# Cross attention on one core: weights five turns behind the scores, four pairs of transposed buffers, contexts loaded in six pieces, the query bias loaded as rows

## The reference

```python
q = (pre_q @ Wq + bq).reshape(b, ql, H, D_Q)          # 16 x 100 x 16 x 64
k = (pre_k @ Wk + bk).reshape(b, kl, H, D_Q)          # 16 x 1444 x 16 x 64
v = (pre_k @ Wv + bv).reshape(b, kl, H, D_Q)
scores = jnp.einsum('bqhd,bkhd->bhqk', q, k) / jnp.sqrt(jnp.float32(D_Q))
attn = jax.nn.softmax(scores, axis=-1)
ctx = jnp.einsum('bhqk,bkhd->bqhd', attn, v).reshape(b, ql, H * D_Q)
out = ctx @ Wo + bo
x = pre_q + out                                       # then a layer norm over the 128 columns
return (x - mu) * jax.lax.rsqrt(var + EPS) * gamma + beta
```

## Time and profile before

| | us |
|---|---|
| median of three runs (lowest, highest) | 870.35 (869.59, 874.36) |
| the profiled execution, its own time | 871.59 |
| its span | 869.8 |
| PE busy in the span | 846.3 (97%) |
| DVE busy | 774.7 (89%) |
| ACT busy | 779.6 (90%) |
| POOL busy | 569.1 (65%) |

### The profile page before, as it was taken

One profiled execution on the slowest core, in us unless ns is written; L12 is line 12 of the kernel. 1 busy time (PEld: TensorE's weight loads), 2 busy tenths in 40 slices (PEclk: granted clock), 3 DMA queues, 4 the chain that ended last, 5 costly groups with the idle time before them and its releaser, 6 DMA issues.

```text
span 869.8 us, 19632 instructions
## 1 busy us (share of the span) xinstructions
PE 846.3 (97%) x7306; PEld 605.2 (70%) x7306; DVE 774.7 (89%) x938; ACT 779.6 (90%) x1132; POOL 569.1 (65%) x575
## 2 busy tenths in 40 slices
PE   7999999999999999999999999999999999999996
PEld 6676776767677766777667776776767777677675
DVE  4988888999989989999899998999899999999984
ACT  5899999989999989999989999998989989999983
POOL 2283997949566693867749586694956669397301
PEclk9999999999999999999999999999999999999999
DMA  7899999999999999999999999999999999999985
GB/s 198 186 211 192 195 210 189 216 200 223 215 209 217 217 204 224 209 226 211 205 213 221 216 208 229 198 227 217 213 215 220 205 233 208 222 188 217 209 183 117
DMA packets 683939, 180.80 MB, mean 208 GB/s; under 512 B 654596, under 2 KB 683076, under 8 KB 683844
## 3 DMA queue, kind: packets, MB, share of 16 engines
q1 hardware_dynamic: 682372, 179.01, 105.7%
q10 hardware_dynamic: 1344, 0.53, 0.3%
q0 software_dynamic: 128, 0.01, 0.0%
HBM read 15.35 MB, written 0.82 MB: 19 GB/s over the span
## 4 chain that ended last, share of the span: by engine, by line
PE 52%; ACT 14%; DVE 13%; DMA 8%; issue 7%; SPq 4%; ACTq 0%; POOLq 0%; POOL 0%; DVEq 0%
PE ps L670 25%; PE ps L631 22%; DMA pt_hi<-p_hi 7%; DVE p_lo L932 6%; ACT p L1072 6%; ACT p_hi L1080 5%; DVE nmax L917 4%; SPq L429 2%; PE ps L495 2%; PE ps L488 2%; SPq L420 1%; ACT unused L1023 1%; DMA bq_pairs<-in_L_xattn_bq_dram 1%; DVE rsum L923 1%; ACT o_t L1110 1%
## 5 line engine op out<-in xcount | busy, mean ns | idle before, releaser
L932 DVE SCALAR_TENSOR_TENSOR p_lo<-p,rinv,p_hi 128x1444 f16<-128x1444 f32 x200 | 370.9, 1855 | 7.5 <-ACT p_hi L1080 7.0
L917 DVE TENSOR_REDUCE nmax<-ps 128x1 f32<-128x1446 f32 x200 | 330.0, 1650 | 18.8 <-PE ps L631 18.3
L1080 ACT ACTIVATE p_hi<-p,rinv 128x1444 f16<-128x1444 f32 x200 | 300.0, 1500 | 32.1 <-DVE rinv L925 28.5
L1072 ACT ACTIVATE p<-ps,nmax 128x1446 f32<-128x1446 f32 x200 | 292.2, 1461 | 17.8 <-DVE nmax L917 15.4
L670 PE MATMUL ps<-pt_hi,c_hi 128*128 128x256 f16 (+1 forms) x1232 | 252.9, 261 | 11.4 <-DMA pt_hi<-p_hi 9.0
L670 PE MATMUL ps<-pt_hi,c_lo 128*128 128x256 f16 (+1 forms) x1232 | 253.0, 261 | 0.0
L631 PE MATMUL ps<-ct_hi,g_hi 128*128 128x482 f16 (+3 forms) x624 | 155.5, 367 | 0.8 <-DVE g_lo L892 0.7
L631 PE MATMUL ps<-ct_lo,g_hi 128*128 128x482 f16 (+3 forms) x624 | 154.9, 366 | 0.0
L631 PE MATMUL ps<-ct_hi,g_lo 128*128 128x482 f16 (+3 forms) x624 | 154.9, 366 | 0.0
L670 PEld LDWEIGHTS ps<-pt_hi,c_hi 128*128 128x128 f16 x1232 | 114.1, 98 | 50.4 <-issue 16.8
L1204 POOL TENSOR_TENSOR g_raw<-g_raw,gb_b 128x400 f32<-128x400 f32 x60 | 81.0, 1350 | 96.2 <-ACT g_raw L1096 96.2
(11 more groups left out here) (138 smaller groups left out, 863.0 us busy)
## 6 DMA issues: line engine op xcount, KB each, us to landing
c_raw<-in_ctx_dram SPq DMA_DIRECT2D x32, 256.0 KB, 6.1
pt_hi<-p_hi SPq DMA_TRANSPOSE x200, 3.5
pt_lo<-p_lo SPq DMA_TRANSPOSE x200, 3.7
c_raw<-in_ctx_dram SPq DMA_DIRECT2D x16, 192.0 KB
c_raw<-in_ctx_dram SPq DMA_DIRECT2D x48, 18.0 KB
out_dram<-late_sb SPq DMA_DIRECT2D x16, 50.0 KB
x_sb<-in_x_dram SPq DMA_DIRECT2D x1, 600.0 KB
o_t<-in_L_xattn_Wq_dram SPq DMA_DIRECT2D x2, 256.0 KB, 4.5
```

The costliest lines, as they stand in the source:

```text
L917: dve.tensor_reduce(nmax[:, n % RING:n % RING + 1], ps[:, bank:bank + 3, 0:KEYW], AX.XY, ALU.max, negate=True).then_inc(s_nm, 1)
L932: dve.scalar_tensor_tensor(out=p_lo[:, n % LOS, 0:KL], in0=p32[:, n % P32S, 0:KL], scalar=rinv[:, i:i + 1], in1=p_hi[:, par, 0:KL], op0=AL ...
L1072: act.activation(p32[:, n % P32S, :].rearrange("p (k w) -> p k w", w=KEYW), ps[:, bank:bank + 3, 0:KEYW], ACT.Exp, bias=nmax[:, i:i + 1], ...
L1080: act.activation(p_hi[:, par, 0:KL], p32[:, n % P32S, 0:KL], ACT.Copy, scale=rinv[:, i:i + 1]).then_inc(s_hi, 1)
```

## The change

- `LAG` goes from 4 to 5: PE weighs a unit one turn later, and ACT takes the result one turn later. `PTS` goes from 3 to 4, a fourth pair of transposed buffers. The loop of PE runs on three turns after the last scores instead of two.
- A context is loaded in `NL` = 6 pieces of `TL` = 2 tiles, at r = 0 to 5 (before: three pieces of four tiles at r = 1 to 3); the three tail copies come with the last piece. Each half has its own semaphore, so that a sum waits for its half alone.
- The places in a window move: `CHI_AT` from (4, 6, 7) to (5, 6, 7), `SUM_AT` from (5, 8) to (8, 9), `TOTAL_AT` from 9 to 10, `STORE_AT` from 2 to 10. The sum over x moves from turns (9, 10) to (4, 10).
- Before the loop: the query bias is loaded as 8 rows of 128 (`bq_rows`), the first DMA on ACT's queue, ahead of Wk; PE transposes it ahead of the weights, and DVE copies it into `bq_pairs`. PE makes the second half of the head products ahead of the bias. ACT empties both of its banks (`J_B` was DVE's); DVE takes over the first x (`J_X`) and `gb_sb` from ACT.

```diff
-    LAG = 4
+    LAG = 5
-    PTS = 3
+    PTS = 4
-    LOADS = 6
+    TL = 2
+    NL = KT // TL
-    LOAD_AT = 1
-    STORE_AT = 2
-    CHI_AT = (4, 6, 7)
+    LOAD_AT = 0
+    STORE_AT = 10
+    CHI_AT = (5, 6, 7)
-    SUM_AT = (5, 8)
-    TOTAL_AT = 9
+    SUM_AT = (8, 9)
+    TOTAL_AT = 10
...
+        bq_rows = sb("bq_rows", [PAIRS, P])
-        s_c = [sem(f"context_loaded{i}") for i in range(2)]
+        s_c = [[sem(f"context_loaded{i}_{half}") for half in range(SUMS)] for i in range(2)]
+        s_bqt = sem("bq_turned")
+        s_bqp = sem("bq_pairs_ready")
-        J_A, J_X, J_B = 4, 6, 7
-        J_G = J_B + 2
+        J_A, J_B, J_X = 4, 6, 8
+        J_G = J_X + 1
-        BY_SCALAR = [1, 3, J_A, J_A + 1, J_X, J_B + 1, J_V1, J_M2]
+        BY_SCALAR = [1, 3, J_A, J_A + 1, J_B, J_B + 1, J_V1, J_M2]
-        X_SUM_AT = (9, 10)
+        X_SUM_AT = (4, 10)
...
+            def load_context(b, i):
+                load_tiles(b, TL * i, TL * (i + 1), s_c[b % 2][i * SUMS // NL])
...
-                if LOAD_AT <= r < LOAD_AT + NT and w + 2 < B:
+                if LOAD_AT <= r < LOAD_AT + NL and w + 2 < B:
...
+            pe.wait_ge(s_bq, 16)
+            pe.transpose(ps[:, JOB_BANK, 0:PAIRS], bq_rows[:, :], ident[0:PAIRS, 0:PAIRS]).then_inc(s_bqt, 1)
...
             head_products_by_two(w_t[0], w_t[1], 0, J_A)
+            pe.wait_ge(s_bqp, 2)
+            head_products_by_two(w_t[0], w_t[1], 2, J_B)
             query_bias(take(J_X))
             spread_context_max(job_bank(J_G + 2), 0)
             transpose_x(0, J_X).then_inc(s_fill, 1)
-            head_products_by_two(w_t[0], w_t[1], 2, J_B)
...
-            for n in range(N + 2):
+            for n in range(N + LAG - 2):
...
+            dve.wait_ge(s_bqt, 1)
+            dve.wait_ge(s_bqz, 1)
+            for i in range(2):
+                rows = slice(HEAD_DIM * i, HEAD_DIM * i + HEAD_DIM)
+                dve.tensor_copy(bq_pairs[rows, :, i], ps[rows, JOB_BANK, 0:PAIRS]).then_inc(s_bqp, 1)
...
-            empty(J_B)
+            empty(J_X)
+            dve.tensor_scalar(gb_sb[:, :], job_bank(J_X)[:, XG * QL:XG * QL + H], SCALE, None, ALU.mult).then_inc(s_gb, 1)
...
+            act.dma_start(bq_rows[:, :], bq.rearrange("(c p) -> c p", p=P)).then_inc(s_bq, 16)
...
-            act.wait_ge(s_bqz, 1)
-            for i in range(2):
-                rows = slice(HEAD_DIM * i, HEAD_DIM * i + HEAD_DIM)
-                act.dma_start(bq_pairs[rows, :, i:i + 1], bq.rearrange("(c i p o) -> i p c o", i=2, p=HEAD_DIM, o=1)[i],
-                              allow_slow_non_contiguous=True).then_inc(s_bq, 16)
...
-            for k in (1, 3, J_A, J_A + 1):
+            for k in (1, 3, J_A, J_A + 1, J_B, J_B + 1):
                 empty(k)
             a_sum(0)
-            empty(J_X)
-            act.activation(gb_sb[:, :], job_bank(J_X)[:, XG * QL:XG * QL + H], ACT.Copy, scale=SCALE).then_inc(s_gb, 1)
```

More of the change, by code:

```diff
@@ L353, in every_other, with context_landed @@
             return slice(first, first + 2 * HG - 1, 2)
-        def context_landed(b):
-            return 16 * LOADS * (b // 2 + b % 2)
+        def context_landed(b, half):
+            return 16 * (NL // SUMS + (3 if half == SUMS - 1 else 0)) * (b // 2 + b % 2)
         def emptied(eng, k):
@@ L371, in _, with load_tiles @@
         def _(sp):
[L372 to L377, removed]
+            def load_tiles(b, a, e, landed):
+                par, whole = b % 2, min(e, KT - 1)
+                sp.dma_start(c_raw[:, par, a:whole, :],
+                             ctx_in[b:b + 1, a * P:whole * P, :].rearrange("o (t p) d -> p (o t) d", p=P)).then_inc(landed, 16)
+                if e == KT:
                     tail = ctx_in[b:b + 1, (KT - 1) * P:KL, :].rearrange("o p d -> p o d")
@@ L386, in _ @@
             for g in range(NT):
-                load_context(0, g)
+                load_tiles(0, TG * g, TG * (g + 1), s_cf[g])
             sp.dma_start(x_sb[:, 0:XG, :], x[0:XG, :, :].rearrange("b q d -> q b d")).then_inc(s_x[0], 16)
@@ L391, in _ @@
                 sp.dma_start(w_raw[2][:, cols], Wv[:, cols]).then_inc(s_w[2][half], 16)
-            for g in range(NT):
-                load_context(1, g)
+            for i in range(NL):
+                load_context(1, i)
             def transpose_context_hi(b):
@@ L539, in query_bias @@
             def query_bias(bank):
-                pe.wait_ge(s_bq, 32)
+                pe.wait_ge(s_bqp, 2)
                 for c in range(PAIRS):
@@ L837, in context_max @@
             def context_max(g):
-                dve.wait_ge(s_cf[g], 16 if g < NT - 1 else 16 * (LOADS - NT + 1))
+                dve.wait_ge(s_cf[g], 16 if g < NT - 1 else 16 * 4)
                 dve.tensor_reduce(c_max[:, g:g + 1], c_raw[:, 0, TG * g:TG * g + TG, :].rearrange("p t d -> p (t d)"),
@@ L1025, in context_sum @@
             def context_sum(b, i):
+                act.wait_ge(s_c[b % 2][i], context_landed(b, i))
                 if i == 0:
-                    act.wait_ge(s_c[b % 2], context_landed(b))
                     act.wait_ge(s_cm, b)
@@ L1038, in a_sum @@
                            ax_parts[:, 0, i:i + 1])
-            for k in (1, 3, J_A, J_A + 1):
+            for k in (1, 3, J_A, J_A + 1, J_B, J_B + 1):
                 empty(k)
             a_sum(0)
-            empty(J_X)
-            act.activation(gb_sb[:, :], job_bank(J_X)[:, XG * QL:XG * QL + H], ACT.Copy, scale=SCALE).then_inc(s_gb, 1)
             for g in range(NT):
                 context_hi(0, g)
-            empty(J_B + 1)
             for g in range(NG):
```

## The result

The changed kernel takes **877.1 us** in the median of 16 runs (870.8 to 883.3), the kernel before 871.8 (869.0 to 876.5) beside it: ratio 1.0054, 95% interval 1.0035 to 1.0074. Timed again later in the study it gave 874.0 beside 871.7, ratio 1.0043 (1.0020 to 1.0066). Ratios leave out slow runs, over 1.5% above the fastest of their kernel, which only two kernels further down have. So the change makes the kernel about 4 us slower. The forecast was 863.2, with a range up to 869.5: the sign was wrong and the time lies outside the range.

The account below looks back on a forecast made before the run. PE was taken as the bound, with 10.4 us of pt_hi waits to gain; -10.4 - 0.8 + 3.2 + 0.5 = -7.5 us gave 862.9, taken as 863.2 us, range 859.5 to 869.5.

Parts of the forecast that it names:

- All 12 stalls go: -10.4 us: Middle of the loop: with LAG 5 and four buffers PE no longer waits for pt_hi, saving 10.4 us.
- the sums' +0.5: Sums at r = 8 and 9: ACT falls back 1.0 us, slack shrinks to nearly nothing; +0.5 us, between 0 and 7.
- What is late next?: Middle, once the stalls are gone: no wait from the four buffer pairs; next is the exponentials' slack, usually least 1.1 us.
- So the lateness is SP's backlog after the loads: Middle: pt_hi comes late because SP issues its transposes late behind other DMAs, not for shortage of ACT or DVE.
- the gain is given back: Rival, middle: late transposes hold ACT's p_hi, PE stalls at its scores, 7 us come back: 869 to 870; chance 0.17.
- Before the loop: -0.8: Start: c_hi and g_lo come sooner, so the first scores do too; -0.8 us, between 0 and -2.0.
- the cover: Before the loop: 1.3 us of PE idle time to absorb weights' transposes starting some 1.2 us late if the rows land late.
- Nothing starts sooner: Turn 4: its 18 matmuls go, but the projection still waits for DVE's scale; 1.97 us of weighing move to the end.
- the clock rival: Rival: TensorE's clock falls behind holes at the end and in turn 4, costing 1.7 to 3.3 us: 864.9 to 866.5; chance 0.15.
- The end, +3.2: After turn 199 starts: PE idles 3.1 us for ACT's copy into o_t, the last unit begins later; +3.2 us.
- Pieces, store and sums at nothing and +0.5: Loop: six load pieces and the moved store cost nothing; sums at r = 8 and 9 cost 0.5 us.
- ACT as the bound: Rival: neighbouring sums and columns at r = 9 delay exponentials past slack; at 1.0 us a window, 876; chance 0.07.

Follow-up runs that it names:

- the combination: Changed kernel with the old start, three p_hi buffers, ACT's last but one copy moved earlier, contexts in three spaced pieces from GpSimd's queue: 863.9 us, ratio 0.9918.

## Why the prediction was wrong, point by point

- **"All 12 stalls go: -10.4 us." Half right.** This term is the step that failed: with the sums' +0.5 the middle was to shorten by 9.9 us and did by 2.2, which is 7.7 of the 11.0 us between the forecast sum (-7.5) and that of the stages (+3.5, below). The stalls for `pt_hi` went. The middle gained 5.0 and 4.4 us in the two profiles of the changed kernel against the one of before. Over five profiles of its loop (798.8 to 802.6, mean 800.2) and three of the loop before (799.7 to 803.9, mean 802.4) the gain is 2.2 us. What the stalls cost was itself read from one profile: a second of the loop before has the same (8.2 us in 12 places of the middle), a third, with the rows behind Wk, 4.7 in 10. The mechanism, and about its size, are borne out by the combination: its middle is 10.8 us shorter than in the profile of the kernel before, 9.3 shorter than the mean of the three. What failed is the question that follows, "What is late next?": it looked at the four pairs of transposed buffers and at the exponentials, and left out the two `p_hi` buffers, which were named only as a rival. In their place the runs show ACT waiting 15.0 us for transposes and PE 4.6 us in the middle for ACT's copy behind it; with a third buffer the first is gone, and in the combination taking it away brings 11.0 us of it back.
- **"So the lateness is SP's backlog after the loads." Half right.** With SP relieved and the pieces spaced, the waits stayed at 7.3 us of 9.0. SP's queue is one part, the landing beside the loads' traffic the other. What the fifth turn gives is room for either.
- **The rival "the gain is given back" (0.17)** had the mechanism: late transposes hold ACT by `p_hi`'s two buffers. It put PE's stall at the scores, for the exponentials; it came at the weighing, for `o_t` (4.6 us of the 6.9 lie in the middle), since ACT's copy stands next behind `p_hi` in its order. Its forecast of 869 to 870 lies 1 to 2 us under the first profiled run and 4 to 8 under the medians, as the start and turn 4 were not in it.
- **"Before the loop: -0.8", bounds 0 to -2.0. Wrong in sign**: +2.1 on the mean of nine profiles each. The step that failed is the bound of 0 for the worst case: nothing in the working made a start slower. What came is the slow pace of the head products in six of nine starts. It weighs more where the change put both halves of them ahead of the bias and the spread of the maximum, and so filled the 1.3 us of idle time that was to be the cover. Overlooked too was what the rows push back. It was asked when they land (they were there by 4.3 us and cost nothing), but they are first on ACT's queue: Wk starts at 1.36 us instead of 0.75, and its second half lands at 7.3 to 9.1 instead of 6.0 to 6.3. Whether this brings the slow pace stays open.
- **"Nothing starts sooner" in turn 4: right, but not free.** The projection started at 38.32 as forecast. The hole of 2.8 us cost 0.2 us where the clock stayed up and 1.9 where it fell behind (12.1 against 10.26 us for turns 4 and 5), which it did in seven of the thirteen profiles with five turns. That is the clock rival, priced at 1.7 and given 0.15. The sum itself gave the hole no cost.
- **The end, +3.2: right in kind**, 0.8 too high; +2.4 measured, with the stall at the place named, 2.29 us for 3.1.
- **Pieces, store and sums at nothing and +0.5: borne out** within what can be measured; undoing pieces and store gave 1.0048 and undoing the sums 1.0044, beside 1.0043 and 1.0054.
- **ACT as the bound (0.07): did not come.** The slower side came by the start, the turn-4 hole and the end instead, +2.1, +1.2 (mean of thirteen) and +2.4, which with -2.2 in the middle make +3.5 us. The two ratios give +3.7 and +4.7. The last us is open: the timed runs of the changed kernel spread over 12 us, and only two of them have a profile.

## What to carry to other kernels

Slack between two engines can be no longer than the fewest buffers on the way allow; here it was the two ahead of the DMA. Before a lag is lengthened, list every buffer from the producer on, those ahead of the DMA too, and lengthen them together. Ask of a small load put first in a queue what it pushes back: here 4 KB of rows moved the start of Wk by 0.6 us and its landing by 1 to 3. Loads moved to a second queue had best keep the spacing and the place that the first gave them; in one burst here they delayed the transfers that someone waited for.

## What the runs showed of the hardware that was not expected

- Six loads of a context issued in a row from GpSimd's queue raised the landing of the transposes on SP's queue from 5.8 to 10.8 us at the longest, with the median unchanged at 3.5, and made the kernel 46 us slower, a part of it by a clock at 0.5 behind the stalls. Spaced over several turns and at another place in the window they cost 4.
- At the start of a run the granted-clock column can stand at 1.00 while TensorE makes its products at half pace, one every 0.21 us for 0.11 (428 ns each for 285). The slow pace has to be read from equal matmuls there. It came in one of the nine old starts and in six of the nine new ones, and in two of these seven the column did show 0.5.
- A stall of 2.8 us of PE in turn 4 was followed by 3.4 to 6.8 us at half the granted clock in seven of the thirteen profiles that have it, and by none in the other six. The same stall costs 0.2, 1.9 or (once) 3.3 us; the times of one kernel mostly lie 5 to 12 us apart, and this spread may be a part of it.
